# Attention chunks and MLP tiles: distance six in place of four, and all weight dequantisation after the first stage

## The chip, the cores and the metric

One core of a Trainium2 chip runs the whole kernel. The time is device microseconds of one execution; the median of three executions of the kernel before is 1163.79 us (1162.48 to 1166.29). Five engines have their own instruction queues and meet only at semaphores: TensorE (PE: matmuls and transposes; its weight loads are listed as PEld), VectorE (DVE), ScalarE (ACT), GpSimd (POOL) and SyncE (SP, here the only queue that issues DMAs).

## The reference, cut to what matters

The input x is 4 x 512 tokens of 512 features in float32.

1. x = x + attention(layernorm(x)). The attention is a gated linear one with 4 heads of 128: q, k, v and two small gates are projections. Tokens go in chunks of 128. In a chunk, y_local = (q k^T * beta * decay) v; across the four chunks of a batch a state of 128 x 128 per head is carried: state = state * total_decay + v^T kw, and y_global = q state * chunk_decay.
2. x = x + mlp(layernorm(x)). Gate and up matrices (4096 x 512) and the down matrix (512 x 4096) are stored as 4-bit codes with one scale per 32 values; they have to be dequantised, then out = (gelu(x Wg) * (x Wu)) Wd.

## The kernel before, in words

**Numbers.** Every matrix product of the projections and the MLP is done in float16 with a high and a low part of each operand, three matmuls in place of one (`XP`). So each operand is written twice: the high part by ACT (a copy), the low part by DVE or POOL (a subtraction).

**First stage (L495 to L517 on PE).** For each of 16 chunks T of 128 tokens the layernorm is computed: DVE takes statistics (`stats`, L809 and L811), POOL forms 1/std (`norm_scale`, L1182 and L1185), DVE writes the normalised tokens (`apply`, L820), PE transposes them (`turn`, L295), ACT copies the high part (L567), DVE subtracts the low part (`turn_low`, L826). PE does eight projections (`qkv`, L327) and the gate logits (L305) between. `apply(T)` stands on DVE behind whatever is ahead of it in DVE's program.

**Attention loop (L518 to L541 on PE).** For each T: `head` (transposes of k, then q k^T), `fills(T)` (up to three projections for later chunks, 12 matmuls each), and `mid` (state product L375, y_local L381, y_global L388; a fourth chunk of a batch, T % 4 == 3, has no state product, a first one no y_global), and `turn("n2", T - 1)`, the transposes of the second layernorm. On DVE: `weigh_keys` (L897, not where T % 4 == 3), `weigh` (L907, which writes `att`, the operand of L381), `apply("n2", T - 1)` (L820), the evictions of the projections, `mid` and `turn_low`.

**MLP tiles.** Tile i (of 128) is 128 hidden units by 512 tokens. `upgate(i)` on PE (L422) is 24 matmuls of 512 columns; ACT takes gelu, DVE multiplies (L957), ACT and DVE or POOL write high and low part. Four tiles make one `down(n, tt)` product (L486), which DVE adds to the output (`gather`, L977). Tiles 0 to 11 run inside the attention loop, tile T - 4 in step T; the down products of tiles 0 to 3 at T = 8, those of tiles 4 to 7 one per step from T = 12, those of 8 to 11 after the loop. From m = 16 on (L552) a different scheme of half-size products is used, which the change leaves alone.

**Weight chunks.** The codes come in 48 weight chunks k, six to a group of 16 tiles (0, 1 gate; 2, 3 up; 4, 5 down). A weight chunk costs DVE `dq_bits` (L983, L986, L988, L991) and `dq_finish` (L1012, twice), then ACT two copies (L670) and POOL two subtractions (L1255). Weight chunk 0 is dequantised in the first stage (DVE at T = 9 and T = 11, POOL behind `norm_scale` of T = 13), weight chunk 1 at its end, weight chunks 2 to 6 in the loop at the steps listed in `DEQUANTED`, 7 after it. In the loop `dq_finish` stands on DVE between `weigh_keys(T)` and `weigh(T)`; `dq_bits` for the next one stands at the end of an earlier step.

**Order.** The order of the work on each engine is written out by hand, once per engine. PSUM banks are handed out in a ring at build time (`Banks`); gate and up of tiles below 12 use one pair of banks, later tiles alternate between two (`pair`).

Of the kernel before, what the change touches and what calls it, by code (L numbers as in the profile page):

```python
# [11 lines left out]
NT = 16  # L12
# [60 lines left out]
    return out  # L73


DEQUANTED = (0, 1, 5, 7, 13)


def nth(i):
# [40 lines left out]
def block_kernel(nc, x, wqkv, bqk, bv, wab, bab, codes, scales, out, cla):  # L120
    with ExitStack() as ctx:
# [75 lines left out]
        PS = [ctx.enter_context(nc.psum_tensor(f"ps{i}", [128, 512], F32)) for i in range(8)]  # L197
# [17 lines left out]
            return ihl_r[:, j] if n >= 3 and n % 2 else ihl_s[:, j]  # L215

        def pair(i):
            return (PS[2], PS[3]) if i < 12 or i % 2 else (PS[4], PS[5])

        def half_bank(kind, name):  # L220
            first = 2 if kind == "gate" else 0
# [59 lines left out]
        def _(eng):  # L281
# [117 lines left out]
            def upgate(i):  # L399
                g, b, j = i // 16, (i % 16) // 4, i % 4  # L400
                buf = WR[g % 2]
                pg, pu = pair(i)
                if i == 12:
                    pe.wait_ge(s_attn, NT)
                    for sm5, value in banks.freed[5]:
                        pe.wait_ge(sm5, value)
                elif i == 13:
                    pe.wait_ge(s_inter, 12)
                elif i >= 12:
                    pe.wait_ge(s_inter, i - 1)  # L410
                elif i >= 1:
                    pe.wait_ge(s_inter, i)
                pe.wait_ge(s_hi["n2"], 4 * b + 4)
                pe.wait_ge(s_lo["n2"], 4 * b + 4)
                for o, bank, kind in ((0, pg, "gate"), (4, pu, "up")):
                    for c in range(2):
                        for nib in range(2):
                            weights(6 * g + o // 2 + c, nib)
                    n = 0
                    for kt in range(4):  # L420
                        for xp, wp in XP:
                            mm = eng.matmul(bank[:, :], buf[:, wp, o + kt, 128 * j:128 * j + 128],  # L422
                                            XT[:, xp, kt, 512 * b:512 * b + 512], start=(n == 0), stop=(n == 11))
                            n += 1
                    mm.then_inc(s_gu[kind], 1)
# [90 lines left out]
            qkv("q", 1, 1)  # L516
            decay(0)  # L517
            for T in range(NT):  # L518
                i, fill = T - 4, fills(T)
                head(T)  # L520
                if T == 0:
                    decay(1)
                for f in fill:
                    qkv(*f)
                if T == 8:
                    for tt in range(4):
                        down(0, tt)
                if T >= 12:
                    down(1, T - 12)
                if i > 0 and i % 4:  # L530
                    upgate(i)
                    turn("n2", T - 1)
                    mid(T)
                elif i >= 0:
                    turn("n2", T - 1)
                    mid(T)
                    upgate(i)
                else:
                    mid(T)
                    if T >= 1:  # L540
                        turn("n2", T - 1)  # L541
            for tt in range(3):
                down(2, tt)
            turn("n2", NT - 1)
            down(2, 3)
            banks.ring = [0, 1, 6, 7]
            for i in range(12, 32):
                upgate(i)
                if i >= 16:
                    down(i // 4 - 1, i % 4)  # L550
            banks.ring = [6, 7]
# [10 lines left out]
        def _(eng):  # L562
# [172 lines left out]
            for T in range(4, NT):  # L735
                if T - 1 in QKV_EARLY:
                    project(*QKV_EARLY[T - 1])
                if T == 5:
                    weights_high(0, range(4))
                turn("n1", T)  # L740
                if T == 12:
                    dequant(0)
            project(*QKV_EARLY[NT - 1])
            dequant(1)
            gates()
            project("q", 1, 0)
            decay(0)
            project("q", 1, 1)
            dk = 2
            for T in range(NT):  # L750
                fill = fills(T)
                norms_of_k(T)
                if T + 1 < NT:
                    decay(T + 1)
                for f in fill:
                    project(*f)
                if T >= 4 and T % 4 == 0:
                    turn("n2", T - 1)
                if T >= 4:
                    act_tile(T - 4)  # L760
                if T % 4:
                    turn("n2", T - 1)
                if T in DEQUANTED:
                    dequant(dk)
                    dk += 1
            turn("n2", NT - 1)
            dequant(7)
            for i in range(12, 32):
                act_tile(i)
# [8 lines left out]
            dk = 16  # L778
# [21 lines left out]
        def _(eng):  # L800
# [265 lines left out]
            for T in range(4, NT):  # L1066
                if T + 1 < NT:
                    stats("n1", T + 1)
                apply("n1", T)
                if T < 6:  # L1070
                    project("v", 0, T - 2)
                if 5 <= T < 8:
                    weights_low(0, [[0, 1], [2], [3]][T - 5])
                if T > 4:
                    turn_low("n1", T - 1)
                if T == 9:
                    dq_bits(0)
                elif T == 11:
                    dq_finish(0)
                elif T == NT - 1:  # L1080
                    dq_bits(1)
            turn_low("n1", NT - 1)
            dq_finish(1)
            gates()
            project("k", 1, 0)
            dq_bits(2)
            dk = 2
            for T in range(NT):
                i, fill = T - 4, fills(T)
                weigh_keys(T)  # L1090
                if T in DEQUANTED:
                    dq_finish(dk)
                    dk += 1
                weigh(T)
                if T >= 1:
                    apply("n2", T - 1)
                for f in fill:
                    project(*f)
                if T == 8:
                    for tt in range(4):  # L1100
                        gather(0, tt)
                if T >= 12:
                    gather(1, T - 12)
                if i > 0 and i % 4:
                    act_tile(i)
                    turn_low("n2", T - 1)
                    mid(T)
                elif i >= 0:
                    turn_low("n2", T - 1)
                    mid(T)  # L1110
                    act_tile(i)
                else:
                    mid(T)
                    if T >= 1:
                        turn_low("n2", T - 1)
                if T in (0, 1, 5, 9):
                    dq_bits(dk)
            apply("n2", NT - 1)
            for tt in range(3):
                gather(2, tt)  # L1120
            turn_low("n2", NT - 1)
            gather(2, 3)
            dq_bits(7)
            dq_finish(7)
            for i in range(12, 32):
                if i == 12:
                    dq_bits(8)
                act_tile(i)
                if i == 12:
                    dq_finish(8)  # L1130
                    dq_bits(9)
                if i == 13:
                    dq_finish(9)
                if i == 15:
                    dq_bits(10)
                if i == 16:
                    dq_finish(10)
                if i == 17:
                    dq_bits(11)
                if i == 18:  # L1140
                    dq_finish(11)
                if 16 <= i < 24 and i % 2:
                    token_sums((i - 16) // 2)
                if i in (21, 23, 27, 29):
                    k = {21: 12, 23: 13, 27: 14, 29: 15}[i]
                    dq_bits(k)
                    dq_finish(k)
                if i >= 16:
                    gather(i // 4 - 1, i % 4)
# [26 lines left out]
        def _(eng):  # L1176
# [139 lines left out]
            eng.tensor_scalar(lower_h[:, :], lower[:, :], 1.0, None, ALU.mult).then_inc(s_setup, 1)  # L1316
            for T in range(NT):
                norm_scale("n1", T)
                if T == NT - 3:
                    dequant(0)  # L1320
            dequant(1)
            gates()
            decay_rows(0)
            decay_rows(1)
            decay_mask(0)
            dk = 2
            for T in range(NT):
                head(T)
                if T + 1 < NT:
                    decay_mask(T + 1)  # L1330
                if T + 2 < NT:
                    decay_rows(T + 2)
                if T >= 4:
                    inter_low(T - 4)
                if T in DEQUANTED:
                    dequant(dk)
                    dk += 1
            norm_scale("n2", NT - 1)
            dequant(7)
            for i in range(12, 32):  # L1340
                inter_low(i)
# [26 lines left out]
        def _(eng):  # L1368
# [41 lines left out]
            load_x(3)  # L1410
            load_chunk(0)
            load_chunk(1)
            load_chunk(2)
            load_chunk(3)
            sp.wait_ge(s_cla, 1)
            eng.dma_start(cla.rearrange("(r c) -> r c", c=128), cla_t).then_inc(s_clout, 16)
            sp.wait_ge(s_clout, 16)
            load_rows(2)
            load_rows(3)
            k = 4  # L1420
            for T in range(NT):
                if 4 <= T + 3 < NT:
                    load_rows(T + 3)
# [47 lines left out]
```

## Time and profile before

| | |
|---|---|
| median of three executions | 1163.79 us |
| the profiled execution | 1163.94 us, of which the span from first to last instruction is 1162.2 us |
| PE busy | 1150.6 us (99%) |
| DVE, ACT, POOL busy | 833.2, 395.9, 504.7 us |
| mean granted TensorE clock | 0.998 |

A timeline row gives start, duration, engine, line, operation, output and input tiles, and in brackets the idle time before it with the instruction that ended it. Consecutive matmuls overlap a little, so the time that a group takes is read from its start to the next start.

### The profile page before, as it was taken

Reading aid. Unit: us, or ns where it says so; the run is one execution under the profiler, and the core shown is the slowest. Engines: PE = TensorE matmul, PEld = TensorE weight load, DVE = VectorE, ACT = ScalarE, POOL = GpSimd, SP = SyncE. Lnnn points to the kernel's source line nnn. Section 1 sums busy time; section 2 is a strip of 40 time slices with the busy share of each in tenths; the row PEclk is TensorE's granted clock in tenths of the full one; section 3 lists DMA queues with packets and bytes.
Section 4 is the critical chain, followed back from the end, with each engine's and each line's share of the span. In section 5 each row is a group of like instructions: output and inputs, shape, how many; then the busy total and the mean of one; then the engine's idle time right before and its main releaser. Section 6 shows DMA issues by size and latency. Waiting matters only on the chain.

```text
span 1162.2 us, 19595 instructions
## 1 busy us (share of the span) xinstructions
PE 1150.6 (99%) x7793; PEld 763.0 (66%) x7793; DVE 833.2 (72%) x1383; ACT 395.9 (34%) x835; POOL 504.7 (43%) x503
## 2 busy tenths in 40 slices
PE   9899999999999999999999999999999999999998
PEld 5566655566544445777777777777777777777775
DVE  7887554555666765987788778777877787777554
ACT  4343432445133232333333333333323333332221
POOL 2376332335255654335633563446344634462110
PEclk9999999999999999999999999999999999999999
DMA  8021010000020010110011001100110010100101
GB/s 298 21 77 35 28 37 10 19 19 19 2 71 1 19 37 19 37 37 20 19 37 38 19 19 37 38 19 19 37 38 21 25 40 27 35 20 11 37 37 64
DMA packets 22683, 41.94 MB, mean 36 GB/s; under 512 B 2688, under 2 KB 2752, under 8 KB 22592
## 3 DMA queue, kind: packets, MB, share of 16 engines
q1 hardware_dynamic: 22592, 40.70, 10.9%
q8 instruction: 61, 1.00, 0.4%
q14 instruction: 30, 0.25, 0.1%
HBM read 36.46 MB, written 4.23 MB: 35 GB/s over the span
## 4 chain that ended last, share of the span: by engine, by line
PE 97%; DVE 1%; POOL 1%; ACT 1%; issue 0%; POOLq 0%; DVEq 0%; ACTq 0%
PE ps L459 38%; PE ps L486 29%; PE ps L422 14%; PE ps L327 9%; PE ps L381 1%; PE ps L295 1%; PE ps L364 1%; PE ps L388 1%; PE ps L375 1%; PE ps L493 1%; PE ps L355 1%; POOL WR L1255 0%; PE ps L305 0%; POOL kn_s L1223 0%; ACT XT L567 0%
## 5 line engine op out<-in xcount | busy, mean ns | idle before, releaser
L486 PE MATMUL ps<-WR,ihl_s 128*128 128x512 f16 x768 | 175.7, 379 | 0.0
L422 PE MATMUL ps<-XT,WR 128*128 128x512 f16 x768 | 170.4, 379 | 0.0
L486 PE MATMUL ps<-WR,vv 128*128 128x512 f16 x720 | 164.7, 379 | 0.0
L459 PE MATMUL ps<-REG,WR 128*128 128x256 f16 x1152 | 157.1, 273 | 0.0
L459 PE MATMUL ps<-XT,WR 128*128 128x256 f16 x1152 | 157.1, 273 | 0.0
L977 DVE SCALAR_TENSOR_TENSOR X<-ps,X 128x512 f32<-128x512 f32 x128 | 88.0, 688 | 75.4 <-PE ps L486 75.4
L459 PEld LDWEIGHTS ps<-XT,WR 128*128 128x128 f16 x1152 | 112.7, 98 | 33.5
L422 PEld LDWEIGHTS ps<-XT,WR 128*128 128x128 f16 x768 | 75.0, 98 | 90.3 <-DVE fw L957 0.9
L486 PEld LDWEIGHTS ps<-WR,ihl_s 128*128 128x128 f16 x768 | 75.2, 98 | 79.7
L459 PEld LDWEIGHTS ps<-REG,WR 128*128 128x128 f16 x1152 | 112.7, 98 | 13.0
L486 PEld LDWEIGHTS ps<-WR,vv 128*128 128x128 f16 x720 | 70.5, 98 | 74.7 <-DVE vv L963 0.2
L1239 POOL TENSOR_TENSOR vv<-fw,vv 128x512 f16<-128x512 f32 x49 | 61.4, 1272 | 119.2 <-ACT vv L646 119.2
L1239 POOL TENSOR_TENSOR ihl_s<-fw,ihl_s 128x512 f16<-128x512 f32 x48 | 60.0, 1270 | 111.6 <-ACT ihl_s L646 111.6
L634 ACT ACTIVATE fw<-load 128x512 f32<-128x512 f32 x96 | 60.5, 631 | 139.2 <-DVE load L1037 134.8
L1255 POOL TENSOR_TENSOR WR<-wf,WR 128x512 f16<-128x512 f32 x48 | 55.9, 1185 | 103.2 <-ACT WR L670 103.2
L719 ACT COPY load<-ps 128x256 f32<-128x256 f32 x48 | 17.9, 372 | 219.5 <-PE ps L459 219.5
L327 PE MATMUL ps<-XT,WR 128*128 128x512 f16 x384 | 87.5, 382 | 0.0
L957 DVE SCALAR_TENSOR_TENSOR fw<-fw,ps 128x512 f32<-128x512 f32 x32 | 21.9, 685 | 73.5 <-PE ps L422 62.5
L957 DVE SCALAR_TENSOR_TENSOR fw<-fw,bigB 128x512 f32<-128x512 f32 x96 | 73.7, 808 | 0.0
L459 PE MATMUL ps<-REG,bigA 128*128 128x256 f16 x576 | 70.7, 273 | 0.0
L1037 DVE TENSOR_TENSOR load<-load,bigB 128x512 f32<-128x512 f32 x48 | 65.7, 1368 | 1.6
L327 PEld LDWEIGHTS ps<-XT,WR 128*128 128x128 f16 x384 | 37.0, 98 | 41.4 <-issue 1.4
(174 smaller groups left out, 1901.2 us busy)
## 6 DMA issues: line engine op xcount, KB each, us to landing
load<-codes SPq DMA_DIRECT2D x48, 256.0 KB
load<-scales SPq DMA_DIRECT2D x48, 256.0 KB
y<-X SPq DMA_DIRECT2D x16, 256.0 KB, 2.0
bigA<-cla SPq DMA_DIRECT2D x14, 256.0 KB, 3.1
X<-x SPq DMA_DIRECT2D x3, 1024.0 KB, 13.2
WR<-wqkv SPq DMA_DIRECT2D x2, 1024.0 KB, 10.1
X<-x SPq DMA_DIRECT2D x4, 256.0 KB, 4.0
WR<-wqkv SPq DMA_DIRECT2D x4, 256.0 KB, 4.4
```

The costliest lines, as they stand in the source:

```text
L295: t = eng.transpose(PS[bank][:, 128 * kt:128 * kt + 128], src, ident[:, :])
L327: mm = eng.matmul(PS[bank][:, :], lhs, rhs, start=(n == 0), stop=(n == 11))
L422: mm = eng.matmul(bank[:, :], buf[:, wp, o + kt, 128 * j:128 * j + 128], XT[:, xp, kt, 512 * b:512 * b + 512], start=(n == 0), stop=(n == 11))
L459: mm = eng.matmul(half_bank(kind, name), w(wp, kt), x(xp, kt), start=(n == 0), stop=(n == 5))
L486: mm = eng.matmul(PS[bank][:, :], ih[:, ip, 128 * tt:128 * tt + 128], buf[:, wp, 8 + j, :], start=(m == 0), stop=(m == 11))
L634: eng.activation(fw[:, i % 2, :], pg, ACT.Gelu_apprx_tanh, scale=GS).then_inc(s_gelu, 1)
L719: eng.copy(even[:, 0:256], half_bank(kind, "P1")).then_inc(s_snap, 1)
L957: eng.scalar_tensor_tensor(w, w, f, pu, ALU.mult, ALU.mult).then_inc(s_inter, 1)
L977: eng.scalar_tensor_tensor(X1[:, T, :], PS[bank_of["dn", n, tt]][:, :], 1.0 / (WS * IS), X1[:, T, :], ALU.mult, ALU.add).then_inc(s_ev, 1)
L1037: eng.tensor_tensor(v[:, :, 256:512], v[:, :, 256:512], s5b.unsqueeze(1).broadcast_to([128, 2, 256]), ALU.add).then_inc(s_comb, 1)
L1239: eng.tensor_tensor(ih[:, 1, :], fw[:, i % 2, :], ih[:, 0, :], ALU.subtract).then_inc(s_ilop, 1)
L1255: eng.tensor_tensor(buf[:, 1, base + nib, :], wf[:, nib, :], buf[:, 0, base + nib, :], ALU.subtract).then_inc(s_wlo, 1)
```

## The change: what it does

MLP tile i moves from step T = i + 4 of the attention loop to step T = i + 6 (`APART`), so tiles 0 to 9 are in the loop and 10 and 11 behind it; inside a step `upgate` now always comes before `turn` and `mid`. The down products follow: tiles 0 to 3 at T = 10, tiles 4 to 7 two at a time at T = 14 and 15, tiles 8 to 11 behind `upgate(12)`. The weight chunks 0 and 1 leave the first stage on all engines; weight chunks 0 to 6 are dequantised in the loop at T = 1, 3, 4, 5, 8, 9, 13. SP asks for two weight chunks ahead of the loop instead of four. The second pair of PSUM banks is used from tile 11 on, by odd tiles. No matmul is added or removed.

```
-DEQUANTED = (0, 1, 5, 7, 13)
+DEQUANTED = (1, 3, 4, 5, 8, 9, 13)
+APART = 6
...
         def pair(i):
-            return (PS[2], PS[3]) if i < 12 or i % 2 else (PS[4], PS[5])
+            return (PS[4], PS[5]) if i > 10 and i % 2 else (PS[2], PS[3])
...
# PE, upgate
-                if i == 12:
+                if i == 11:
                     pe.wait_ge(s_attn, NT)
                     for sm5, value in banks.freed[5]:
                         pe.wait_ge(sm5, value)
-                elif i == 13:
-                    pe.wait_ge(s_inter, 12)
...
# PE, loop
             for T in range(NT):
-                i, fill = T - 4, fills(T)
+                i, fill = T - APART, fills(T)
                 head(T)
...
-                if T == 8:
+                if T == 10:
                     for tt in range(4):
                         down(0, tt)
-                if T >= 12:
-                    down(1, T - 12)
-                if i > 0 and i % 4:
+                if T >= 14:
+                    down(1, 2 * T - 28)
+                    down(1, 2 * T - 27)
+                if i >= 0:
                     upgate(i)
                     turn("n2", T - 1)
                     mid(T)
-                elif i >= 0:
-                    turn("n2", T - 1)
-                    mid(T)
-                    upgate(i)
                 else:
                     mid(T)
                     if T >= 1:
                         turn("n2", T - 1)
-            for tt in range(3):
-                down(2, tt)
+            upgate(NT - APART)
             turn("n2", NT - 1)
-            down(2, 3)
             banks.ring = [0, 1, 6, 7]
-            for i in range(12, 32):
+            for i in range(NT - APART + 1, 32):
                 upgate(i)
+                if i == 12:
+                    for tt in range(4):
+                        down(2, tt)
...
# DVE, first stage and loop (ACT and POOL in the same way)
-                if T == 9:
-                    dq_bits(0)
-                elif T == 11:
-                    dq_finish(0)
-                elif T == NT - 1:
-                    dq_bits(1)
             turn_low("n1", NT - 1)
-            dq_finish(1)
             gates()
             project("k", 1, 0)
-            dq_bits(2)
-            dk = 2
+            dk = 0
...
-                if T in (0, 1, 5, 9):
+                if T + 1 in DEQUANTED:
                     dq_bits(dk)
             apply("n2", NT - 1)
-            for tt in range(3):
-                gather(2, tt)
+            act_tile(NT - APART)
             turn_low("n2", NT - 1)
-            gather(2, 3)
+            act_tile(NT - APART + 1)
             dq_bits(7)
             dq_finish(7)
...
# POOL, first stage
-                if T == NT - 3:
-                    dequant(0)
-            dequant(1)
...
# SP
             load_chunk(1)
-            load_chunk(2)
-            load_chunk(3)
...
-            k = 4
+            k = 2
```

## Rows read from the trace of the kernel before

**Rows 1.** The page, busy time by engine.

```profile
PE 1150.6 (99%) x7793; PEld 763.0 (66%) x7793; DVE 833.2 (72%) x1383; ACT 395.9 (34%) x835; POOL 504.7 (43%) x503
```

**Rows 2.** PE's waits, whole span: waited for, us in total, times, longest.

```profile
PE ps L295 <- DVE bigA L820: 4.2, 2, 2.3
...
PE ps L381 <- DVE bigB L907: 0.4, 2, 0.2
```

**Rows 3.** Two stretches: busy time by engine, then PEclk, DMA share, GB/s.

```profile
40.00:60.00 20.00, 16.46 (x145) 10.03 (x146) 16.00 (x32) 7.27 (x14) 6.95 (x13) 0.91 0.09 27
...
100.00:150.00 50.00, 50.00 (x283) 29.26 (x282) 31.66 (x58) 19.80 (x46) 24.56 (x38) 1.00 0.11 32
```

**Rows 4.** Timeline of PE, first stage.

```profile
41.65 1.11 PE L295 MATMUL ps<-bigC,bigA 128*128 128x128 f32 x4 [2.27 <-DVE bigA L820]
...
42.92 3.65 PE L327 MATMUL ps<-XT,WR 128*128 128x512 f16 x12
...
47.92 2.75 PE L327 MATMUL ps<-XT,WR 128*128 128x512 f16 x12
...
53.28 0.65 PE L295 MATMUL ps<-bigC,bigA 128*128 128x128 f32 x4 [1.89 <-DVE bigA L820]
```

**Rows 5.** Timeline of DVE, first stage.

```profile
38.12 0.68 DVE L983 SCALAR_TENSOR_TENSOR load<-load 128x512 int32<-128x512 int32 x1
...
40.24 0.69 DVE L809 BATCH_NORM_STATS2 bst<-X 128x6 f32<-128x512 f32 x1
...
41.06 0.53 DVE L820 TENSOR_SCALAR bigA<-X,mv,rs 128x512 f32<-128x512 f32 x1
...
52.68 0.55 DVE L820 TENSOR_SCALAR bigA<-X,mv,rs 128x512 f32<-128x512 f32 x1 [1.65 <-POOL rs L1185]
```

**Rows 6.** Timeline of POOL, first stage.

```profile
49.29 2.45 POOL L1255 TENSOR_TENSOR WR<-wf,WR 128x512 f16<-128x512 f32 x2 [2.03 <-ACT WR L670]
```

**Rows 7.** Timeline of DVE, attention chunks 0 to 3.

```profile
73.79 2.56 DVE L1012 SCALAR_TENSOR_TENSOR wf<-tb,load 128x512 f32<-128x512 f16 x2
...
80.32 0.66 DVE L983 SCALAR_TENSOR_TENSOR load<-load 128x512 int32<-128x512 int32 x1
...
82.45 0.68 DVE L897 TENSOR_TENSOR bigB<-ps,kn_s 128x512 f32<-128x512 f32 x1
83.05 1.52 DVE L1012 SCALAR_TENSOR_TENSOR wf<-tb,load 128x512 f32<-128x512 f16 x2
84.50 0.68 DVE L907 TENSOR_TENSOR bigB<-ps,bigB 128x512 f32<-128x512 f32 x1
85.10 0.77 DVE L820 TENSOR_SCALAR bigA<-X,mv,rs 128x512 f32<-128x512 f32 x1
...
101.61 0.66 DVE L826 TENSOR_TENSOR XT<-ps,XT 128x512 f16<-128x512 f32 x1
103.14 0.69 DVE L907 TENSOR_TENSOR bigB<-ps,bigB 128x512 f32<-128x512 f32 x1 [0.88 <-POOL bigB L1229]
```

**Rows 8.** Timeline of PE: attention chunk 3, and MLP tile 1.

```profile
98.17 0.60 PE L355 MATMUL ps<-bigC,REG 128*128 128x128 f32 x4
...
104.68 1.05 PE L381 MATMUL ps<-vv,bigB 128*128 128x128 f32 x8
...
132.57 5.34 PE L422 MATMUL ps<-XT,WR 128*128 128x512 f16 x24
```

**Rows 9.** Timeline of DVE, end of attention chunk 5.

```profile
139.33 0.69 DVE L963 TENSOR_TENSOR ihl_s<-fw,ihl_s 128x512 f16<-128x512 f32 x1 [0.69 <-ACT ihl_s L646]
...
144.27 0.66 DVE L983 SCALAR_TENSOR_TENSOR load<-load 128x512 int32<-128x512 int32 x1
...
147.21 0.68 DVE L897 TENSOR_TENSOR bigB<-ps,kn_s 128x512 f32<-128x512 f32 x1
```

**Rows 10.** Timeline of PE behind the attention loop.

```profile
303.20 7.93 PE L486 MATMUL ps<-WR 128*128 128x512 f16 x36
```

**Rows 11.** Timeline of DVE behind the attention loop.

```profile
307.47 0.55 DVE L820 TENSOR_SCALAR bigA<-X,mv,rs 128x512 f32<-128x512 f32 x1 [0.96 <-POOL rs L1185]
```

More of the change, by code:

```diff
@@ L740, in _ @@
                 turn("n1", T)
-                if T == 12:
-                    dequant(0)
             project(*QKV_EARLY[NT - 1])
-            dequant(1)
             gates()
@@ L756, in _ @@
                     project(*f)
[L757 to L761, printed above, removed]
+                if T >= APART:
+                    act_tile(T - APART)
+                if T >= 1:
                     turn("n2", T - 1)
@@ L1075, in _ @@
                     turn_low("n1", T - 1)
-                if T == 9:
-                    dq_bits(0)
-                elif T == 11:
-                    dq_finish(0)
-                elif T == NT - 1:
-                    dq_bits(1)
             turn_low("n1", NT - 1)
-            dq_finish(1)
             gates()
             project("k", 1, 0)
-            dq_bits(2)
-            dk = 2
+            dk = 0
             for T in range(NT):
-                i, fill = T - 4, fills(T)
+                i, fill = T - APART, fills(T)
                 weigh_keys(T)
@@ L1098, in _ @@
                     project(*f)
-                if T == 8:
+                if T == 10:
                     for tt in range(4):
                         gather(0, tt)
-                if T >= 12:
-                    gather(1, T - 12)
-                if i > 0 and i % 4:
+                if T >= 14:
+                    gather(1, 2 * T - 28)
+                    gather(1, 2 * T - 27)
+                if i >= 0:
                     act_tile(i)
@@ L1107, in _ @@
                     mid(T)
[L1108 to L1111, printed above, removed]
                 else:
@@ L1115, in _ @@
                         turn_low("n2", T - 1)
-                if T in (0, 1, 5, 9):
+                if T + 1 in DEQUANTED:
                     dq_bits(dk)
             apply("n2", NT - 1)
-            for tt in range(3):
-                gather(2, tt)
+            act_tile(NT - APART)
             turn_low("n2", NT - 1)
-            gather(2, 3)
+            act_tile(NT - APART + 1)
             dq_bits(7)
@@ L1129, in _ @@
                 if i == 12:
+                    for tt in range(4):
+                        gather(2, tt)
                     dq_finish(8)
@@ L1318, in _ @@
                 norm_scale("n1", T)
-                if T == NT - 3:
-                    dequant(0)
-            dequant(1)
             gates()
@@ L1325, in _ @@
             decay_mask(0)
-            dk = 2
+            dk = 0
             for T in range(NT):
@@ L1332, in _ @@
                     decay_rows(T + 2)
-                if T >= 4:
-                    inter_low(T - 4)
+                if T >= APART:
+                    inter_low(T - APART)
                 if T in DEQUANTED:
@@ L1338, in _ @@
             norm_scale("n2", NT - 1)
+            inter_low(NT - APART)
+            inter_low(NT - APART + 1)
             dequant(7)
```

## The prediction

> **What bounds the kernel now.** I read the page first: PE is busy for 1150.6 of 1162.2 us [rows 1], so 11.6 us of idle time and whatever the clock takes are all that a reordering can win back. No matmul is added or removed, so the whole case is about where PE waits, and when. PE's waits come next [rows 2]: one group matters, the transposes L295 behind DVE's `apply` L820, 4.2 us in two waits; the waits for `weigh` L907 are 0.4 us. The stretches tell where, and show a third loss: from 40 to 60 us PE is busy for 16.46 of 20 us at a granted clock of 0.91, which is about 3.6 us at half rate (1.2 in place of 2.4 GHz); from 100 to 150 us it is busy for 50.00 of 50 [rows 3], and so in every stretch up to the tail. The timeline then gives the places: the waits end at 41.65 and 53.28 us, and the clock is low right behind the idle of 2.27 us, where the transposes take 1.11 us against 0.65 and the projection behind them 3.65 against 2.75 [rows 4]. That is 1.4 us lost. DVE, POOL and ACT set nothing there; they only have to keep their dates. So the change can win about 5.6 us in the first stage, and it can lose wherever DVE gets more work inside a step in which PE has less.
>
> **What it removes.** (a) The wait at 41.65 us. DVE has `dq_bits(0)` from 38.12 us to the statistics at 40.24, 2.12 us, ahead of `apply(10)` at 41.06 [rows 5]. Without it `apply(10)` starts at 38.94 and ends at 39.47; PE, free at 41.65 - 2.27 = 39.38 [rows 4], waits 0.15 us in place of 2.27: gain 2.1 us. What is late next is the same engine: for each attention chunk DVE has statistics, `apply` and a low part, about 1.9 us, two chunks for every 4.1 us of PE (a projection of 2.6 and two transposes with logits). It keeps up with little to spare.
> (b) The clock. If it falls because PE stood still, it doesn't fall now: 1.4 us.
> (c) The wait at 53.28 us. `apply(14)` at 52.68 waited 1.65 us for POOL's 1/std [rows 5], and POOL had the two subtractions of weight chunk 0 at 49.29, 2.45 us [rows 6]. They go. I leave 0.2 us of wait here, since DVE is nearly full: gain 1.7 us.
> (d) `dq_bits(1)` and `dq_finish(1)` ahead of the gates stood in DVE's idle time (the gates wait for PE's logits): nothing. `dq_bits(2)` ahead of the loop likewise, but `dq_finish` at T = 0 (2.56 us, at 73.79 [rows 7]) stands ahead of `weigh(0)` and goes: with a little at chunk 2, where POOL runs beside less DVE work, I take 0.4 us, all of the second line of [rows 2].
> Sum of gains: 2.1 + 1.4 + 1.7 + 0.4 = 5.6 us (bounds 4.5 and 5.9).
>
> **What it adds.** Seven weight chunks are dequantised in the loop in place of five, and the steps 4 and 5 lose their MLP tile. I took every step and asked whether `weigh_keys`, `weigh` and `apply` meet PE's date.
> (e) Chunk 3. PE's step is `head`, two projections, then y_local L381, which needs `weigh(3)`: start 98.17, date 104.68, 6.51 us later [rows 8]. DVE ends the low part of chunk 1 at 101.61 + 0.66 = 102.27, and before it only waited for POOL until 103.14 [rows 7]. Now `dq_bits(1)` (end of step 2) and `dq_finish(1)` (step 3) both stand there: 2.13 + 1.45 = 3.58 us by the sequence at 80.32 to 84.50 without its L897 (82.45 to 83.05) [rows 7]. `weigh(3)` starts at 105.85, ends at 106.53, and with 0.06 us for the semaphore (41.59 to 41.65 in [rows 4, 5]) PE goes on at 106.6: a new wait of 1.9 us. Bounds: `dq_bits` 2.1 to 2.94 (144.27 to 147.21 [rows 9]), `dq_finish` 1.2 (two instructions at the 0.6 us from 84.50 to 85.10) to 2.56 [rows 7]: 1.7 to 3.8 us. Behind it apply(2), the evictions and PE's `turn(2)` are in time.
> (f) By the same durations (estimates): chunks 4 and 5 have three projections (9.1 us up to the state product, 10.0 to y_local). DVE comes to `weigh_keys(4)` some 5.5 us into the step and is through `dq_finish` and `weigh` at 7.5 to 8.8; in chunk 5 POOL's two subtractions stand ahead of its norm of k, which puts `weigh(5)` at 8.3. Both meet their date by over 1 us: nothing. Steps 6 to 11 last 17.4 us or more: nothing.
> (g) Chunk 13. Before, its step had a down product ahead of the transposes of L295; now it has `head`, `upgate(7)` and at once `turn(12)`, which needs `apply(12)`. Date: 1.33 + 5.18 = 6.51 us into the step (24 matmuls at 0.216 us; `head` is 98.17 to 99.50) [rows 8]. DVE: in step 12 the low part of tile 6 starts 1.58 us behind the end of `upgate` (137.75 to 139.33) [rows 8, 9]; it and four more of about 0.67 us follow (low part, state, sum, statistics), so `dq_bits(6)` starts 4.93 us behind that end, and PE's next step begins 0.47 + 2 x 0.89 = 2.25 us behind it: 2.7 us into the step. From there bits, `weigh_keys`, finish and `weigh` take 4.78 us (80.32 to 85.10), `apply` 0.77 [rows 7]: 8.2 us, a wait of 1.8 us. Bounds: with the short forms (1.2 for the finish) 8.0, with the long ones (2.7 + 2.94 + 0.6 + 2.56 + 0.6 + 0.77) 10.2: 1.5 to 3.7 us. Here the instruction that waits is a transpose, and y_local, the head of chunk 14 and its down products are queued behind it; all move by the same time.
> (h) Behind the loop. `turn(15)` needs `apply(15)`, which came 4.8 us behind the end of `mid(15)` (303.20 to 308.02) [rows 10, 11]. It was covered by three down products, 7.8 us; now by `upgate(10)`, 5.18 us. It holds, by 0.4 us; without that cover it would cost up to 0.5. Weight chunks 8 and 9 wait for down(2), now one tile later, and are needed three tiles after it: some 7 us of room. The PSUM ring gives `upgate(11)` bank 5 last used by `turn(14)`, long read. Steady state from tile 13 on: unchanged.
> (i) SP: `load_chunk(k)` waits for `dq_finish(k - 2)`, with the rows of the decay behind it; each is used more than one step later. Nothing.
>
> A row and a rule on how long (e) and (g) are: `dq_bits` took 2.13 us at 80.32 and 2.94 at 144.27, and the longer one ran beside POOL instructions [rows 7, 9]. The Trainium skill (SBUF — State Buffer, Who interferes with whom) says that an instruction of VectorE in a two-port mode and one of GpSimd lock a shared port pair in turn, and the later one blocks for the whole of the other. By that rule POOL's decay work of chunks 3 and 13 would stand in the way of the two TENSOR_SCALAR instructions, and each wait would be nearer to its upper bound, about 2.8 us; the time would be 1163.9.
>
> **Sum.** The profiled execution: span 1162.2, time 1163.94, so 1.74 us lie around the span. 1162.2 - 5.6 + 1.9 + 1.8 = 1160.3, and with 1.74 the time is 1162.0. The profiled time is 0.15 us over the median, so I leave it. That is 0.15% less than before. A change of 0.3%, 3.5 us, is about what a measurement can tell from none: limits 1160.3 and 1167.3.
>
> **Rivals.**
> A: the new waits don't come, or one only, because DVE or POOL run ahead of what I think (DVE had 0.88 us idle ahead of `weigh(3)` [rows 7], and steps may drift apart). Then 1163.94 - 5.6 = 1158.3, with one wait 1160.2. Against: both sums exceed the date with the shortest forms too. Chance 0.26.
> B, slower: contention of DVE and POOL makes both waits long. 3.8 + 3.7 = 7.5 us, and each is then over the 2.27 us after which the clock was halved [rows 3, 4], 1.4 us each: 1163.94 - 5.6 + 7.5 + 2.8 = 1168.6. It decides from the point where the two waits with their clock cost over 9 us. For it: 2.56 us for a `dq_finish` beside POOL; against: such rows are the rarer. Chance 0.12.
> C: the first stage gives less, since DVE is nearly full there and PE meets it a chunk later: 3 us in place of 5.2: 1164.2. Against: without the eight instructions DVE has about 0.3 us to spare per pair. Chance 0.12.
> D, part of the forecast: one of the two waits passes 2.27 us or the clock falls after a shorter one: 1163.4.
>
> **How the numbers follow.** Forecast with D 0.50 (1160.4 to 1164.8), A 0.26, B 0.12, C 0.12. Faster by over 0.3% is A and a little of the forecast, 0.29; slower by over 0.3% is most of B, 0.10; the rest, 0.61, within. The range leaves out the lower half of A and the upper half of B: 1158.6 to 1166.8.
>
> **What would show it.** In the changed kernel: no wait of L295 over 0.5 us and a clock of 1.00 before 60 us; the gates (the waits for their table of exponentials, now near 64 us) reached about 5 us earlier; PE waits for L907 about 2 us in chunk 3, and for L820 about 2 us once in chunk 13 (near 270 us); no wait in chunks 4, 5 or behind the loop. The forecast is wrong if either new wait is missing, or over 3 us, or if PE's idle time leaves the first stage by less than 3 us.

## The result

The changed kernel takes 1166.74 us (median of 14 runs, 1164.05 to 1168.28), the kernel before 1164.24 us beside it (14 runs). The ratio is 1.0020 (95% interval 1.0013 to 1.0027): 0.2% slower. Forecast were 1162.0 us, 0.15% faster, with a range of 1158.6 to 1166.8. The time lies in the range, 0.06 us below its upper end, and under the 0.3% that the forecast called no change, but on the other side of the kernel before.

### The profile page after: what moved, and what is told of

It reads as the page before. It is cut to its first block, busy times and chain, and to the rows that moved or that the text cites. A ratio compares the mean times of both kernels' runs of the same rounds, so it can differ in the third digit from the quotient of the medians.

```text
span 1166.5 us, 19592 instructions
## 1 busy us (share of the span) xinstructions
PE 1152.6 (99%) x7793; PEld 765.3 (66%) x7793; DVE 833.7 (71%) x1383; ACT 390.2 (33%) x831; POOL 507.8 (44%) x503
## 4 chain that ended last, share of the span: by engine, by line
PE 95%; DVE 3%; POOL 1%; issue 1%; ACT 0%; DVEq 0%; POOLq 0%; ACTq 0%
PE ps L458 38%; PE ps L485 28%; PE ps L421 14%; PE ps L328 8%; PE ps L382 1%; PE ps L296 1%; PE ps L389 1%; PE ps L365 1%; PE ps L376 1%; PE ps L356 0%; PE ps L492 0%; DVE XT L820 0%; POOL WR L1239 0%; DVE wf L1006 0%; DVE bst L803 0%
```

## The profile after

The profiled execution took 1168.28 us (span 1166.5 us, 4.3 more than before), the slowest of the 14. The page shows the same 7793 matmuls as [rows 1], with PE busy 2 us longer:

```profile
PE 1152.6 (99%) x7793; PEld 765.3 (66%) x7793; DVE 833.7 (71%) x1383; ACT 390.2 (33%) x831; POOL 507.8 (44%) x503
```

PE's waits (us in total, times, longest), beside [rows 2]. `apply` is now L814, `weigh` L901, y_local L382:

```profile
PE ps L382 <- DVE bigB L901: 3.5, 1, 3.5
PE ps L296 <- DVE bigA L814: 2.4, 1, 2.4
PE ps L492 <- POOL bigC L1293: 1.8, 1, 1.8
PE ps L328 <- DVE XT L820: 1.1, 1, 1.1
```

The two waits of the first stage are gone, two new ones are in the attention loop. The stretches (busy time of PE, PEld, DVE, ACT, POOL; then PEclk, DMA share, GB/s), beside [rows 3]:

```profile
40.00:60.00 20.00, 19.72 (x199) 11.91 (x197) 12.77 (x34) 8.42 (x17) 4.95 (x11) 1.00 0.01 2
100.00:120.00 20.00, 18.84 (x106) 14.11 (x107) 16.27 (x29) 6.10 (x22) 10.41 (x12) 0.83 0.22 66
260.00:280.00 20.00, 17.62 (x97) 11.56 (x95) 12.20 (x24) 7.08 (x16) 8.78 (x13) 0.91 0.09 27
```

The first is what was forecast: a granted clock of 1.00 and 3.3 us more busy time than before. In the other two the clock falls: a mean that is 0.17 below full over 20 us is about 6.8 us at 1.2 in place of 2.4 GHz, 0.09 is about 3.4 to 3.6 us. "PE busy" hides this, since matmuls at half clock take longer and count as busy all that time: the eight of L382 below took 2.05 us in place of 1.05. PE's timeline of the first stage, beside [rows 4]:

```profile
39.08 0.66 PE L296 MATMUL ps<-bigC,bigA 128*128 128x128 f32 x4
...
47.59 0.66 PE L296 MATMUL ps<-bigC,bigA 128*128 128x128 f32 x4
```

They are the transposes of chunks 10 and 14, 0.15 us behind the logits before them in both cases (forecast: 0.15 and 0.2). Attention chunk 3 and chunk 13, beside [rows 8]:

```profile
94.89 2.75 PE L328 MATMUL ps<-WR,XT 128*128 128x512 f16 x12
101.16 2.05 PE L382 MATMUL ps<-vv,bigB 128*128 128x128 f32 x8 [3.52 <-DVE bigB L901]
103.00 1.91 PE L389 MATMUL ps<-bigA,REG 128*128 128x128 f32 x8
...
107.54 5.34 PE L328 MATMUL ps<-XT,WR 128*128 128x512 f16 x24
...
255.10 5.34 PE L421 MATMUL ps<-XT,WR 128*128 128x512 f16 x24
262.83 0.74 PE L296 MATMUL ps<-bigC,bigA 128*128 128x128 f32 x4 [2.38 <-DVE bigA L814]
263.41 1.47 PE L376 MATMUL ps<-vv,bigB 128*128 128x128 f32 x8
264.67 1.91 PE L382 MATMUL ps<-vv,bigB 128*128 128x128 f32 x8
```

y_local could have started at 94.89 + 2.59 = 97.48 and started at 101.16: 3.7 us. The eight products behind it took 1.84 us to the next start. In the kernel before they took 0.89, from 104.68 [rows 8] to this row:

```profile
105.57 1.06 PE L388 MATMUL ps<-bigA,REG 128*128 128x128 f32 x8
```

From 101.16 to 107.54 are 6.38 us for work of 3.6 (104.68 to 108.27 before): another 2.8. At chunk 13 the transposes were due at 255.10 + 5.18 = 260.28 and came at 262.83 (2.55 us), and half clock behind them cost 1.7.

DVE in front of `weigh(3)`, beside [rows 7], and POOL at the same time:

```profile
94.41 0.66 DVE L820 TENSOR_TENSOR XT<-ps,XT 128x512 f16<-128x512 f32 x1
94.99 1.41 DVE L977 SCALAR_TENSOR_TENSOR load<-load 128x512 int32<-128x512 int32 x1
96.43 0.43 DVE L980 TENSOR_SCALAR tb<-load 128x512 int32<-128x512 int32 x1
96.78 0.42 DVE L982 TENSOR_SCALAR load<-load 128x512 int32<-128x512 int32 x1
97.23 0.69 DVE L985 TENSOR_TENSOR tb<-tb,load 128x512 int32<-128x512 int32 x1
97.96 2.46 DVE L1006 SCALAR_TENSOR_TENSOR wf<-tb,load 128x512 f32<-128x512 f16 x2
100.34 0.68 DVE L901 TENSOR_TENSOR bigB<-ps,bigB 128x512 f32<-128x512 f32 x1
```

```profile
94.81 1.04 POOL L1213 TENSOR_TENSOR bigB<-bigB,kn_s 128x512 f32<-128x512 f32 x1
...
97.26 1.17 POOL L1196 TENSOR_SCALAR_AFFINE_SELECT bigB<-bigB 128x512 f32<-128x512 f32 x1
98.40 1.47 POOL L1190 TENSOR_TENSOR bigA<-bigA,bigD 128x512 f32<-128x512 f32 x1
```

There is no idle time on DVE: low part, `dq_bits(1)`, `dq_finish(1)`, `weigh(3)`, one after the other. The first instruction of `dq_bits` took 1.41 us, beside POOL's L1213 on 128x512 (in [rows 7], at 80.32, it took 0.66, beside a POOL instruction on 128x4 only), and `dq_finish` 2.38 to the next start.

**A ledger from the start times of the same instructions**, after against before, in the profiled runs:

| PE reaches | before | after | difference |
|---|---|---|---|
| the sums of the gates | 64.45 | 58.40 | -6.05 |
| y_local of chunk 0 | 77.10 | 70.44 | -6.66 |
| the head of chunk 3 | 98.17 | 90.97 | -7.20 |
| y_local of chunk 3 | 104.68 | 101.16 | -3.52 |
| the first projection of chunk 4 | 108.27 | 107.54 | -0.73 |
| the last output sum (DVE) | 1158.65 | 1162.23 | +3.58 |

0.45 us of the first difference was there at 35 us already, ahead of all that the change touches (35.13 against 34.68), and is not its gain. Between the last two lines lie 4.3 us. Chunk 13 has 4.25 of them (2.55 of waiting, 1.7 of clock). Chunk 5 adds 0.26 (a small wait of y_global), and some 0.2 us come back at a place that I did not look for.

## Experiments

Two theories. **Placement**: the two new waits come from where weight chunks 1 and 6 stand on DVE, and the half clock from PE standing still in them. **Rival**: the steps without an MLP tile, or with less projection work, are too short whatever is in them (the distance of six is to blame), and the clock falls for another reason. Each kernel ran beside the kernel before, whose median there was 1164.1 to 1164.4 us; each ratio is to that one.

**1. Chunk 3 cleared (c3).**

```
-DEQUANTED = (1, 3, 4, 5, 8, 9, 13)
+DEQUANTED = (0, 1, 4, 5, 8, 9, 13)
 # DVE, ahead of the loop
+            dq_bits(0)
```

> Weight chunks at steps 0, 1, 4, 5, 8, 9, 13: only the two at steps 1 and 3 move, so that nothing is dequantised ahead of weigh(3). Placement theory: the 3.7 us wait ahead of y_local in attention chunk 3 and the 2.8 us of half clock behind it go, some 0.6 us come back at chunk 0 (dq_finish(0) ahead of weigh(0)); the wait of 2.5 us at chunk 13 stays: 1166.7 - 6 = about 1161, 3 us below before. Rival (the step is simply too short without its MLP tile, whatever stands in it): the wait at chunk 3 stays over 2 us, time 1165 or more.

Measured: 1160.76 us (9 runs), ratio 0.9972 (0.9963 to 0.9982). The wait at chunk 3 is gone, that of 2.38 us at chunk 13 is there. Placement holds: PE's step 3 is as short as in the changed kernel, but DVE has nothing of the dequantisation ahead of `weigh(3)`.

**2. Chunk 13 cleared (c14).**

```
-DEQUANTED = (1, 3, 4, 5, 8, 9, 13)
+DEQUANTED = (1, 3, 4, 5, 8, 9, 14)
```

> Weight chunk 6 at step 14 in place of 13, nothing else. Placement theory: the wait of L296 at chunk 13 falls from 2.4 us to under 0.3 and the clock stays full there; step 14 has two down products ahead of its transposes and hides the same DVE work: 1166.7 - 4.0 = about 1162.7. Rival: the wait moves to step 14 (turn(13) or the down products waiting for tile 7), time unchanged within 1 us.

Measured: 1163.06 us (11 runs), ratio 0.9993 (0.9984 to 1.0002): 3.7 us under the changed kernel, not told apart from the one before. The wait at chunk 13 is gone and none took its place in chunk 14.

**3. Both (both, and both_b once more on another chip).** `DEQUANTED = (0, 1, 4, 5, 8, 9, 14)`.

> Both moves: steps 0, 1, 4, 5, 8, 9, 14. Placement theory: no wait over 0.5 us from the gates to the end and a granted clock of 1.00 up to the tail; what is left is the gain of the first stage, 6 to 7 us: 1157 to 1158. Rival: the waits come back in other steps (chunk 1 or 2 full, or chunk 4): 1160 or more.

> The kernel with the weight chunks at steps 0, 1, 4, 5, 8, 9, 14 once more, beside the two others: 1157.8 again within 0.5 us, 0.5% below before; the rival, a lucky chip, would have it at 1160.

Measured: 1157.82 us (1157.32 to 1158.80), ratio 0.9947 (0.9934 to 0.9959), and the second time 1157.81 us, 0.9943 (0.9931 to 0.9956). PE's waits, all in the first 17 us, as in the changed kernel:

```profile
PE ps L492 <- POOL bigC L1294: 1.8, 1, 1.8
PE ps L328 <- DVE XT L820: 1.1, 1, 1.1
PE ps L328 <- issue: 0.2, 1, 0.2
```

This version beats both kernels: 6.3 and 6.6 us under the one before, the gain of the first stage without the two waits. All ten runs had a mean clock of 1.000.

**4. The same waits, but PE busy in them (warm).**

```
 # PE, ahead of the wait for weigh(3)
+                if T == 3:
+                    for _ in range(32):
+                        eng.transpose(PS[2][:, 0:128], ident[:, :], ident[:, :])
 # PE, turn("n2", 12), ahead of the wait for apply(12): 20 such transposes
```

> The changed kernel with idle work of PE inside its two new waits: 32 transposes (3.5 us) ahead of the wait of y_local in chunk 3, 20 (2.2 us) ahead of the transposes of chunk 13; they fit into the waits and write where nothing is read. Theory that standing still lowers the clock: the waits keep their length (same date of weigh(3) and apply(12)), the clock stays at 1.00 behind both, time 1166.7 less 2.8 and 1.7 for runs that had both, about 1163 in the median. Rival (the clock falls for another reason, e.g. the float32 products of the loop): the clock falls at the same places and the time stays 1166 to 1167.

Measured: 1163.90 us (11 runs), all with a clock of 0.999 or 1.000. PE's timeline:

```profile
97.45 3.66 PE L387 MATMUL ps<-bigC 128*128 128x128 f32 x32
101.03 1.16 PE L390 MATMUL ps<-vv,bigB 128*128 128x128 f32 x8
102.02 1.06 PE L397 MATMUL ps<-bigA,REG 128*128 128x128 f32 x8
...
257.50 2.35 PE L294 MATMUL ps<-bigC 128*128 128x128 f32 x20
260.06 0.74 PE L301 MATMUL ps<-bigC,bigA 128*128 128x128 f32 x4 [0.20 <-DVE bigA L822]
260.64 1.06 PE L381 MATMUL ps<-vv,bigB 128*128 128x128 f32 x8
```

y_local starts where it did (101.03), but its eight products take 0.99 us to the next start in place of 1.84. So the 2.8 us between the two medians (1166.74 and 1163.90) are the clock, and standing still in these two waits is what lowers it. What is left, 1163.9 against 1157.8, is the waiting: 6.1 us, where the profiled run has 3.7 + 2.55 = 6.25.

**5. The distance alone (dist).** Weight chunks 0 and 1 stay in the first stage, `DEQUANTED` and the places of `dq_bits` are those of before; only `APART = 6` and what hangs on it.

> Distance of six alone: weight chunks 0 and 1 stay in the first stage as before, 2 to 6 at steps 0, 1, 5, 7, 13 as before. Theory: no gain in the first stage (the two waits near 41 and 53 us and the clock at 0.91 there are back), no new wait at chunk 3, but the one at chunk 13 of about 2.4 us with 1.7 us of half clock: 1164.2 + 4 = about 1168. Rival (the distance itself brings the gain): under 1164.

Measured: 1165.38 us (10 runs), ratio 1.0009 (0.9999 to 1.0019). Both waits of the first stage are back, as expected, and the distance brings no gain. But 1168 was a miss: chunk 13 waits only

```profile
261.58 0.74 PE L296 MATMUL ps<-bigC,bigA 128*128 128x128 f32 x4 [0.68 <-DVE bigA L817]
```

0.68 us, because here `dq_bits(6)` stands at the end of step 9 as before, and only `dq_finish(6)` in step 13. I had overlooked that in writing this expectation. It splits the wait of 2.38 us: the difference of 1.7 goes with `dq_bits` in the step right before.

**6. The dequantisation alone (near).** The kernel before, distance four, with `DEQUANTED = (0, 1, 2, 3, 5, 7, 13)` and nothing of it in the first stage.

> The dequantisation alone: distance four as before, weight chunks 0 to 3 at steps 0 to 3, so that they are there for tile 0 in step 4; nothing in the first stage. Theory: the first stage gains its 6 us, but steps 2 and 3 have 4 us of DVE work too much: a wait at chunk 3 of 4 to 7 us with 1.7 to 3.4 us of half clock: 1164 to 1169. Rival (DVE has room for it at any distance): about 1158.

Measured: 1163.77 us (10 runs), ratio 0.9996 (0.9987 to 1.0005). The gain of the first stage goes back into two waits for `weigh`, at chunks 2 and 3:

```profile
91.72 1.13 PE L381 MATMUL ps<-vv,bigB 128*128 128x128 f32 x8 [1.17 <-DVE bigB L904]
...
103.13 1.13 PE L381 MATMUL ps<-vv,bigB 128*128 128x128 f32 x8 [2.41 <-DVE bigB L904]
```

I had expected one of 4 to 7 us at chunk 3; the two together are 3.6 us, and the clock was full behind both in this profile. This kernel is 6 us slower than both. So the distance of six is no gain by itself, but it is what lets weight chunks 2 and 3 wait until steps 4 and 5.

**7. The smallest repair (early).** The changed kernel with `dq_bits(1)` at the end of step 1, where DVE waited 2.4 us for POOL, and weight chunk 6 at step 14.

```
-                if T + 1 in DEQUANTED:
+                if T in (0, 1, 3, 4, 7, 8, 13):
                     dq_bits(dk)
```

> The changed kernel with dq_bits(1) at the end of step 1 in place of step 2, where DVE waited 2.4 us for POOL, and weight chunk 6 at step 14. dq_finish(1) stays in step 3. Theory: only the sum of dq_bits and dq_finish made DVE late; dq_finish alone (1.2 to 2.5 us from 95.0) ends before the date of y_local (97.5 us) but for up to 0.7 us: wait at chunk 3 under 0.7 us, clock full, 1157 to 1158.5. Rival (dq_finish ahead of weigh(3) is enough to be late, or dq_bits in step 1 delays chunk 2): wait over 1.5 us at chunk 2 or 3, over 1159.5.

Measured: 1158.67 us (5 runs), ratio 0.9951 (0.9939 to 0.9964).

```profile
95.60 2.75 PE L328 MATMUL ps<-WR,XT 128*128 128x512 f16 x12
98.45 1.13 PE L382 MATMUL ps<-vv,bigB 128*128 128x128 f32 x8
```

y_local is 0.26 us late, with `dq_finish(1)` still ahead of `weigh(3)`. So `dq_finish(1)` alone (1.93 us here) hardly makes DVE late; with `dq_bits(1)` ahead of it in the same step it does. `dq_bits(1)` alone was not run.

**8. Whose 2.4 us (lean).** The changed kernel with POOL's mask of chunk 4 and rows of chunk 5 done on 4 of 128 columns per head: it leaves out the rest, so the attention of those chunks is not computed properly.

```
+                w = 4 if T == 5 else 128
-                    row = h4(rows[:, T % 2, :])
+                    row = h4(rows[:, T % 2, :])[:, :, 0:w]
 # and the affine_select of decay_mask(4) in the same way
```

> The changed kernel with two POOL instructions of step 3 cut to 4 of 128 columns per head (the mask of chunk 4 and the rows of chunk 5), so their output is wrong there; they ran beside dq_finish(1), which took 2.4 us. Port theory (POOL's instructions hold DVE's up): dq_finish(1) falls to 1.2 to 1.5 us, the wait of y_local in chunk 3 from 3.5 to about 2.5 us, with the clock half for 3.4 in place of 6.8 us in most runs: 2 us less than 1166.7. Rival (dq_finish takes that long by itself): wait and time unchanged.

Measured: 1164.50 us (10 runs). DVE, POOL and PE:

```profile
98.47 1.31 DVE L1006 SCALAR_TENSOR_TENSOR wf<-tb,load 128x512 f32<-128x512 f16 x2
99.70 0.68 DVE L901 TENSOR_TENSOR bigB<-ps,bigB 128x512 f32<-128x512 f32 x1
```

```profile
97.77 0.75 POOL L1198 TENSOR_SCALAR_AFFINE_SELECT bigB<-bigB 128x16 f32<-128x16 f32 x1
98.50 0.73 POOL L1191 TENSOR_TENSOR bigA<-bigA,bigD 128x16 f32<-128x16 f32 x1
```

```profile
100.52 1.13 PE L382 MATMUL ps<-vv,bigB 128*128 128x128 f32 x8 [2.35 <-DVE bigB L901]
101.49 1.06 PE L389 MATMUL ps<-bigA,REG 128*128 128x128 f32 x8
```

`dq_finish(1)` takes 1.23 us in place of 2.38, the wait falls from 3.52 to 2.35 us, and in this profile the clock stays full behind it. The median is 2.2 us less: 1.2 us is the shorter wait, and the rest goes with the clock (mean 0.997 to 0.999 in place of 0.995 to 0.998 in 13 of 14 runs). L977 still takes 1.41 us, since its neighbour L1213 was not cut: that this neighbour holds it up is read from the timeline, and no run tests it.

**9. The clock in the kernel before (before_warm, before_warm2).** 20 transposes of filler in the wait at 41 us; then 18 there and 16 in the one at 53 us.

> The kernel before with 20 transposes (2.2 us) of idle work on PE inside its wait of 2.27 us near 40 us. Theory that standing still lowers the clock: no fall of the clock at 41 us, the wait's end where it was, 1.4 us less: about 1162.8. Rival: clock and time as before, 1164.2.

> The kernel before with idle work of PE in both waits of the first stage: 18 transposes ahead of turn(10), 16 ahead of turn(14). In the kernel with only the first wait filled about half the runs still had a clock of 0.998 and 1164.9. Theory (the second wait of 1.9 us can lower the clock as well): all runs at 0.999 to 1.000 and about 1162.7 to 1163.3. Rival (the half clock of those runs is elsewhere): the same mix of 1162.7 and 1164.9.

Measured: 1163.68 us (12 runs), ratio 0.9996 (0.9988 to 1.0005), five runs still at a clock of 0.998 and 1164.9 to 1165.1 us: less than expected, not told apart from no change. With both filled 1163.08 us (11 runs), ratio 0.9989 (0.9980 to 0.9997), every run at 0.999 or 1.000. So the half clock of the kernel before comes from these two waits, and filling them is worth 1.3 us in the median (0.3 to 2.3). The waits are not the same with the filler: where the kernel before had none, PE, no longer slowed, now waits for `apply`, and that takes back half of the 1.4 us of clock in the profiled run. In before_warm:

```profile
46.85 0.66 PE L298 MATMUL ps<-bigC,bigA 128*128 128x128 f32 x4 [0.67 <-DVE bigA L823]
```

## Why the prediction was wrong, point by point

**In short.** The places and the causes of the new waits were right. The step that failed is the size of (e) and (g), and with it the clock behind them, which the sum put at nothing. Forecast were 1.9 + 1.8 = 3.7 us of waiting and no loss of clock; measured were 3.7 + 2.55 = 6.25 us of waiting in the profiled run and 2.8 us of clock in the median. That is 5.4 us more. The gain was 1.1 us more than forecast and hides a part of it: -6.7 + 6.25 + 2.8 = +2.3 us, measured +2.5. That the time still fell inside the range is luck of this kind, two errors that partly cancel.

**(a), (c) The waits of the first stage.** Right, to 0.1 us: 0.15 us of wait left in each place. **(b)** The clock there is full, and before_warm2 shows that it was the standing still; its worth is about 1.3 us in the median.

**(d) What is gained at chunks 0 to 2.** Taken at 0.4 us, measured 1.15 (-6.05 to -7.20). Nothing now stands ahead of `weigh(0)` (0.3 us), and `decay(1)` and chunk 2 come 0.3 and 0.5 us earlier; that less dequantisation on DVE and POOL does it is likely, but no run shows it. Together the gain was about 6.7 us, not 5.6.

**(e) The term that failed.** Place and cause were right: `dq_bits(1)` and `dq_finish(1)` stand without a gap ahead of `weigh(3)`, and PE waits for L901. The size was off: 3.58 us by the sequence of chunk 1, measured 94.99 to 100.34 = 5.35 us; the wait 3.7 us, not 1.9, at the upper bound of 3.8. Of the 1.77 us of difference 0.84 is `dq_bits` (2.97 for 2.13) and 0.93 `dq_finish` (2.38 for 1.45). I took one favourable row for each and did not ask what POOL does at that moment. The kernel before had a third row of `dq_bits`, at the end of step 1, with its first instruction held up beside POOL (2.76 us in all, from 90.69 to the end of its last instruction at 93.45):

```profile
90.69 1.24 DVE L983 SCALAR_TENSOR_TENSOR load<-load 128x512 int32<-128x512 int32 x1
```

```profile
89.11 2.27 POOL L1255 TENSOR_TENSOR WR<-wf,WR 128x512 f16<-128x512 f32 x2 [2.34 <-ACT WR L670]
```

The prediction also reads the two rows of `dq_bits` as one with and one without POOL beside it; both had POOL beside them, but the shorter one (80.32) at first only its instruction on 128x4. lean shows that 1.15 of the 2.38 us of `dq_finish` are due to POOL's two instructions. The Trainium skill's rule on the shared port pair (SBUF — State Buffer, Who interferes with whom), which the prediction weighed against the row, also names VectorE instructions with two SBUF inputs against a GpSimd instruction that reads SBUF; L977 and L1006 are such, L1213, L1196 and L1190 on the other side, and the trace agrees (1.41 against 0.66 us, 2.38 against 1.23). The two TENSOR_SCALAR instructions that the prediction named were not held up in chunk 3 (0.43 and 0.42 us). Nor does every such pair block for the whole instruction: in chunk 13 L977 took 0.66 us at 256.44, although POOL's L1207 on 128x4, 1.04 us long, had started at 255.95.

**(g) Chunk 13.** 1.8 us forecast, 2.55 measured, in the right place; the same error, smaller: `dq_bits(6)` began 2.7 us into the step as forecast, but took 2.83 us (256.44 to 259.27) in place of 2.13. **(f), (h), (i)** held, but for 0.26 us in chunk 5; there is no wait behind the loop.

**The sum, and the clock.** The forecast charged the clock only beyond 2.27 us of standing still, and put both waits below. Both were above, and the clock cost 2.8 + 1.7 = 4.5 us in the profiled run, and 2.8 us in the median, by warm. The limit itself was no limit either: 2.27 us was only the one wait behind which that profile showed the fall, and before_warm, with that wait filled, still has five runs in twelve at 0.998, and before_warm2 puts that down to the second wait (1.89 us in the kernel before, 1.43 in the profiled run of before_warm). So waits of 1.8 and 1.9 us, as forecast, could have cost clock in some runs too. Without the clock the changed kernel is level with the one before (1163.9 against 1164.1). The runs show it by themselves: the one with a clock of 1.000 took 1164.05 us, those at 0.997 some 1166.4 to 1167.2, the two at 0.995 1167.7 and 1168.3.

**The rivals.** B (contention, two long waits, the clock behind both: 1168.6) was the mechanism that came, at a lesser price than its own since (g) stayed in the middle and the first stage gave more. It had a chance of 0.12. I hold that too low, since its condition, POOL at work beside DVE, could be read off the timeline. A and C did not come. The chances by size (0.61 for within 0.3%) were borne out, the sign was not.

## What to carry to other kernels

Work that moves into a step with slack is not paid by its sum but by its place: ask for each date (here `weigh` and `apply`) what stands on the feeding engine between the last thing that it waits for and the date, and price that with what runs on its neighbour at that moment. The same seven weight chunks cost 9 us more or less (1166.7 against 1157.8) by moving three of them by one or two steps. A wait of PE can cost more than its length, because of the clock behind it; where it can't be removed, filler transposes in it win the clock back (2.8 us here for 52 of them).

## What was unexpected of the hardware

A wait of 3.52 us was followed by about 6.8 us at 1.2 GHz in the profiled run of the changed kernel and one of 3.50 us by about 3.4 us in that of c14. Waits of 2.4 us were followed by about 3.4 us at half clock in some profiles (the changed kernel and lean, chunk 13) and by none in others (c3 at chunk 13, near and lean at chunk 3). So the length of the wait alone does not decide it; what else does stays open. The changed kernel spreads over 4.2 us from run to run, and its time goes with the mean clock. The version without waits of this size (both) spreads over 1.5 us.
